# Ternary feed-forward stages: the sums of squares of a half block enter the matmul with ones as one piece

## The reference, cut to what matters

```python
def _ternary_linear(x, w):
    ...
    rms = jnp.sqrt(jnp.sum(x * x, axis=-1, keepdims=True)) / jnp.sqrt(jnp.asarray(d, x.dtype))
    x_norm = x / (rms + EPS)
    return jnp.einsum('bsd,fd->bsf', x_norm, w_q)
h = jax.nn.gelu(_ternary_linear(x, w_up), approximate=False)
return _ternary_linear(h, w_down)
```

## Time and profile before

| | us |
|---|---|
| median of 3 runs | 1459.81 (1459.66 to 1461.78) |
| the profiled execution | 1459.51 |
| its span, first to last instruction | 1457.6 |
| granted TensorE clock, mean | 0.994 |
| PE busy | 1405.6 (96%) |
| VectorE busy | 1059.7 (73%) |
| ScalarE busy | 927.1 (64%) |
| GpSimd busy | 809.0 (55%) |

### The profile page before, as it was taken

How to read it: one execution, slowest core, us unless ns; L and a number is a source line. 1 busy time by engine, 2 the same in 40 slices (tenths; PEclk the granted TensorE clock), 3 DMA queues, 4 the chain that set the end, 5 groups by cost and what they waited for, 6 DMA issues and landing times. The chain is left out here.

```text
span 1457.6 us, 36349 instructions
## 1 busy us (share of the span) xinstructions
PE 1405.6 (96%) x13004; PEld 1169.9 (80%) x13004; DVE 1059.7 (73%) x2347; ACT 927.1 (64%) x1872; POOL 809.0 (55%) x884
## 2 busy tenths in 40 slices
PE   6999999999998999999999999998899999989998
PEld 5777877889896788888889888887677777768886
DVE  6877777565546887776664669775899999966775
ACT  4665565565552655555655558776778887767775
POOL 3766666322113657665552437776666666636774
PEclk9999999999999999999999999999999999999999
DMA  7000000100001000000311010000000000000101
GB/s 228 31 2 1 0 1 2 37 1 1 1 1 58 2 2 1 0 2 2 103 43 29 1 41 1 1 0 1 2 2 0 0 0 0 0 2 10 36 29 44
DMA packets 21176, 26.28 MB, mean 18 GB/s; under 512 B 1984, under 2 KB 19136, under 8 KB 20928
## 3 DMA queue, kind: packets, MB, share of 16 engines
q1 hardware_dynamic: 20768, 24.61, 5.2%
q10 hardware_dynamic: 288, 0.07, 0.0%
HBM read 20.48 MB, written 4.19 MB: 17 GB/s over the span
## 5 line engine op out<-in xcount | busy, mean ns | idle before, releaser
L548 DVE TENSOR_TENSOR ffn_h_lo<-ffn_h,ffn_h_hi 128x512 fp32r<-128x512 f32 x112 | 86.2, 770 | 122.2 <-ACT ffn_h_hi L759 122.2
L758 ACT ACTIVATE ffn_h<-ffn_hp,c_b 128x512 f32<-128x512 f32 x112 | 77.3, 690 | 145.2 <-PE ffn_hp L857 144.7
L548 DVE TENSOR_TENSOR ternary_ffn_h_lo<-ternary_ffn_h,ternary_ffn_h_hi 128x512 fp32r<-128x512 f32 x128 | 110.8, 865 | 76.4 <-ACT ternary_ffn_h_hi L759 76.3
L2218 POOL TENSOR_TENSOR win_rms<-win_sq_sum,win_minus_half 128x20 f32<-128x20 f32 x31 | 109.8, 3540 | 65.0 <-DVE win_sq_sum L2333 65.0
L1253 POOL TENSOR_TENSOR ret_qk<-ret_qk,ret_qk_sin 128x512 f32<-128x512 f32 x64 | 82.7, 1292 | 99.4 <-DVE ret_qk_sin L1360 98.7
L870 PE MATMUL ternary_ffn_yp<-down_ternary,ternary_ffn_h_hi 128*128 128x256 f32 x512 | 132.4, 291 | 0.0
L870 PE MATMUL ternary_ffn_yp<-down_ternary,ternary_ffn_h_lo 128*128 128x256 f32 x512 | 127.7, 282 | 0.0
L870 PE MATMUL ffn_yp<-down_hi,ffn_h_hi 128*128 128x256 f32 x448 | 127.5, 285 | 0.0
L1259 POOL TENSOR_TENSOR ret_rstd<-ret_sums,ret_minus_half 128x16 f32<-128x16 f32 x32 | 103.7, 3240 | 42.7 <-DVE ret_sums L1402 42.7
L870 PE MATMUL ffn_yp<-down_hi,ffn_h_lo 128*128 128x256 f32 x448 | 125.0, 279 | 0.0
L870 PE MATMUL ffn_yp<-down_lo,ffn_h_hi 128*128 128x256 f32 x448 | 125.0, 279 | 0.0
(11 more groups left out here) (331 smaller groups left out, 4683.0 us busy)
## 6 DMA issues: line engine op xcount, KB each, us to landing
staging<-in_w SPq DMA_DIRECT2D x4, 1024.0 KB, 6.1
ffn_x_in<-in_x SPq DMA_DIRECT2D x8, 512.0 KB, 3.7
X<-in_x SPq DMA_DIRECT2D x7, 512.0 KB, 8.0
out<-X SPq DMA_DIRECT2D x7, 512.0 KB, 2.9
staging<-in_wqkv SPq DMA_DIRECT2D x2, 768.0 KB, 4.5
rotary<-in_rotary SPq DMA_DIRECT2D x1, 1024.0 KB, 6.8
staging<-in_w_up SPq DMA_DIRECT2D x1, 1024.0 KB, 5.1
staging<-in_w_down SPq DMA_DIRECT2D x1, 1024.0 KB, 7.6
```

The lines of the kernel that those rows point to most:

```text
L548: nc.vector.tensor_tensor(h_lo[:, m % R, :], h[:, m % R, :], h_hi[:, m % R, :].bitcast(F32), ALU.subtract).then_inc(h_ready, 1)
L758: nc.scalar.activation(h[:, m % R, :], hp[m % 2][:, :], fn, bias=bias)
L2218: nc.gpsimd.tensor_tensor(rms[:, 1, :], sq_sum[:, :], minus_half[:, :], ALU.pow).then_inc(rms_work, 1)
```

## The change

PE no longer takes the two pair sums of a half. VectorE adds them once more, piece 2 into 0 and piece 6 into 4 (`add_halves`), and PE multiplies one piece by ones instead of two: four matmuls in place of eight. The first half's addition stands in VectorE's order after `h_lo` of piece 4 of the same block; the second's after `h_lo` of piece 0 of the next iteration, ahead of `normalise`. PE waits for the new semaphore `halves_added` where it waited for `sq_added`. The second half of a stage's last block is as it was.

```diff
@@ -175,6 +175,7 @@
         w_summed, w_added, total_done = sem("w_summed"), sem("w_added"), sem("total_done")
         limit_done, below_done, made = sem("limit_done"), sem("below_done"), sem("made")
         mix_first, mix_whole, mix_high, ones_set = sem("mix_first"), sem("mix_whole"), sem("mix_high"), sem("ones_set")
+        halves_added = sem("halves_added")
         lo_done, gain_set = sem("lo_done"), sem("gain_set")
         qkv_full, raw_done, sq_done, values_done = sem("qkv_full"), sem("raw_done"), sem("sq_done"), sem("values_done")
         sq_sum_done, head_work, head_scaled = sem("sq_sum_done"), sem("head_work"), sem("head_scaled")
@@ -548,6 +549,13 @@
                 nc.vector.tensor_tensor(h_lo[:, m % R, :], h[:, m % R, :], h_hi[:, m % R, :].bitcast(F32),
                                         ALU.subtract).then_inc(h_ready, 1)
 
+            def add_halves(b, half):
+
+                dve.wait_ge(sq_added, 4 * b + 2 * (half + 1))
+                m = MF // 2 * half
+                nc.vector.tensor_tensor(h_sq[:, m, :], h_sq[:, m, :], h_sq[:, m + 2, :], ALU.add
+                                        ).then_inc(halves_added, 1)
+
             def input_low(b, j, k):
                 dve.wait_ge(xt_read, KD * b + j + 1)
                 full = tp[j][:, :] if ternary else xt[:, j, :]
@@ -711,6 +719,10 @@
                             residual(b - 2, k)
                         if to_do(b):
                             hidden_low(b, m)
+                        if m == 4 and ternary and live(b, NB):
+                            add_halves(b, 0)
+                        if m == 0 and ternary and live(b - 1, NB) and not final_block(b - 1):
+                            add_halves(b - 1, 1)
                         if m == 1 and first_after_begun(g):
                             normalise(g - 1, 1 - k)
                         if m == 0 and ternary and fresh(g - 1):
@@ -894,8 +906,8 @@
                     pe.wait_ge(pool_sq, POOL_SQ * (b + 1))
                     pieces = (4, 5, 6, 7) if adds_late(b) else (4, 6, 7)
                 else:
-                    pe.wait_ge(sq_added, 4 * b + 2 * (half + 1))
-                    pieces = (4 * half, 4 * half + 2)
+                    pe.wait_ge(halves_added, 2 * b + half + 1)
+                    pieces = (4 * half,)
                 if half == 0:
                     at_least(pe, ms_done, b)
                     if at_start(b):
```

## The result

The changed kernel takes 1462.88 us (median of 20 runs, 1461.29 to 1463.80), the kernel before 1459.88 in the same sitting: a ratio of 1.0019, 95% interval 1.0013 to 1.0025. That is 3.0 us slower by the medians, a hair over the 2.9 us that the prediction counted as the same, and 0.19% by the ratio. The interval excludes no change, so this is a small loss and not a draw. The forecast was 1459.9 in a range of 1455.2 to 1464.0. The profiled execution took 1462.72 us with a span of 1460.9, 3.2 us above the one before.

The account below looks back on a forecast made before the run. PE was taken to bound the steady ternary blocks (17.49 us). -6.6 us gain, +3.1 early blocks and +3.9 full blocks gave +0.4 on 1459.51, so 1459.9 us, range 1455.2 to 1464.0.

Parts of the forecast that it names:

- no change that can be told: Whole kernel: stalls and gain cancel to within 2.9 us, 1459.9 us forecast; chance 0.47.
- Two waves a group: PE's 30 record groups: each loses two waves of 0.11 us, 0.22 us a group, 6.6 us won.
- The m = 4 addition costs nothing: First half's addition on VectorE: its wait is empty and it fits idle time of 1.18 us, so no cost.
- Three early blocks: Three blocks where PE already waits for xt_lo: VectorE sets the pace, 1.04 us lost each, 3.1 us together.
- Seven full blocks: Blocks with all the VectorE work: pair sum catches xn and later work stalls PE, 0.55 us each, 3.9 together.
- my worked case of 0.8: Upper bound for a full block, with xn, h_lo and xt_lo delayed by GpSimd: some 0.8 us of stall.
- GpSimd keeps losing: Rival 1: in the seven blocks GpSimd loses each race, no stall, 1456.0 us, floor 1452.9; chance 0.27 with floor.
- Rival 2: VectorE stays late block to block through h_lo 7, 1.82 us instead of 0.69; four blocks add 4.5, 1464.4 us; chance 0.22.
- one wave: Rival 3: PE's groups shorten by only one wave, 0.11 us less a group, 3.3 less won, 1463.2 us; chance 0.04.
- The smallest difference that can be told: Whole kernel's time: a difference under 0.2% (2.9 us) can't be told from none.

Follow-up runs that it names:

- experiment 4: Changed kernel, but GpSimd's first pair sum adds only 8 of 512 columns, so most of piece 1's squares are missing: 1455.85 us, ratio 0.9969.
- experiment 5: Changed kernel without either addition: PE multiplies one piece per half and most pair sums go unadded, so squares are missing: 1458.43 us, ratio 0.9988 against the kernel before.
- experiment 1: Changed kernel with only the first half's addition (m = 4); the second half goes to PE as two pieces: 1458.97 us, ratio 0.9994.
- experiment 6: Only the first half's addition, as in experiment 1, but block 0 of the first ternary stage done as before (two pieces): 1456.54 us, ratio 0.9978.
- experiment 8: Changed kernel, but the additions write a tile of their own and PE waits for them yet still multiplies two pieces: 1464.13 us, ratio 1.0029.
- experiment 3: Changed kernel with the second half's addition one step later, at m = 1, behind xn and h_lo of piece 1: 1463.92 us, ratio 1.0028.
- experiment 7: Experiment 3 with PE asking for the second half's sum one step later (m = 4 in place of 3): 1459.43 us, ratio 1.0001.
- experiment 11: Experiment 5, but block 0 of the first ternary stage keeps two pieces per half: 1458.48 us, ratio 0.9988 against the kernel before.

## Why the prediction was right, and where not

The time lies in the range, 3.0 us above the value, but "no change that can be told" didn't hold: the interval starts at 1.0013. Luck has a part in how near it came. The term for PE's gain is right only where VectorE has slack, the term for the stalls was too small, and of the 3.3 us between the two spans some 1.4 are not the change's.

*Two waves a group, 6.6 us.* The size was right: 296 records in groups of 8, 0.35 us from the group to what follows (0.57 before), 0.44 a block in experiment 4's steady blocks. That PE keeps this once won was the silent premise, and experiment 5 refutes it: alone it is worth 1.5 us. I had asked what VectorE's lateness brings on, and only in one sentence what PE's earliness does.

*The m = 4 addition costs nothing.* Right in steady blocks (17.26 or 17.27 us in experiment 1). In block 0 of the first stage, where VectorE has the weights to prepare, the edit costs 1.5 to 2.4 us by way of block 1 (experiments 1 and 6). Whether that is the addition's price or that of PE's shorter group isn't shown: either alone comes with a long block 1 (20.2 us in experiment 8, 19.8 in experiment 5). I had counted that block as an early one but looked for the cost only in the m = 0 addition.

*Three early blocks, +3.1.* By blocks: first stage 20.21 for 18.16 and 17.42 for 18.01; second 18.20 for 17.49, and 17.26 for 18.01. The sum of the first pair is +1.46 where I had +1.2 (2 x 1.04 less the 0.44 of each); of the second -0.04 where I had +0.16. The total is near, the shape not: the loss falls on one block, and the next gets part of it back. What made block 1 of the first stage long is `h_lo` 2 at 1.77 us, which the sum doesn't name.

*Seven full blocks, 0.55 each.* The mechanism was right in its places: `xn` caught, `h_lo` 1 to its limit, `h_lo` 2 behind the square of piece 3, `xt_lo` late. The size is the term that was too small: 17.78 less 17.05 is 0.73 us, close to my worked case of 0.8 and not to my value; 7 x 0.18 = 1.3 us of the miss, and the last block of the first stage (17.96) adds 0.2. I had counted on races that come out differently from block to block. In the changed kernel they don't: 17.77 or 17.78 us repeats. (In experiments 3, 7 and 8 they alternate.) The `xn` groups show what the Trainium skill ("SBUF — State Buffer", section "SBUF: two separate sides") says: the engine that starts first holds the shared port pair and the other "fully blocks". The trace agrees, 1.39 us to 2.36 with the pair sum from 1386.96 to 1388.35.

*The rest of the 2.8 us between forecast and profile.* The first stage's start, first up matmul to first transposes, took 6.4 us at a granted clock of 0.74, 5.4 at 1.00 before. The change isn't its cause: it is 6.3 at 0.73 in experiment 11, which has no addition, and 5.4 at 1.00 in experiment 8, which has all. 0.4 lie between the stages. Both are differences of single executions; how often the 20 runs had either start is not known, so that the change's own share of the 3.0 us between the medians is not exactly known; between the two profiles it is about 1.9.

*Rivals.* 1 (GpSimd keeps losing): refuted by `xn` at 2.36. 2 (lateness carried from block to block): the carrying is real, and in experiment 5's first stage through the very link I named, `h_lo` 7 at 1.66 us. In the changed kernel `h_lo` 7 takes 0.69 us in the steady block of 1381.86; the circle closes through `xn` and `h_lo` 2 instead, at a lower price than 1.13. 3 (one wave): refuted. Rival 2's price was summed for four blocks, while "from the third of the seven on" would be five.

*The smallest difference that can be told.* Taken as 0.2% from three runs. With 20 runs the interval is 0.06% to either side.

## What to carry to other kernels

Where two engines hold each other up, an edit's cost is not its duration but the phase it gives to what stands behind it: list the instruction pairs that lie within some tenths of a microsecond of a collision, and move time on either engine only with that list. A block that gets shorter on the bounding engine moves every engine's requests forward, and can lose the gain by itself. Of two symmetrical edits try each alone: here one half was free in steady blocks and the other cost more than both gained. Leave out the odd block too, as its neighbours' work differs: doing block 0 of one stage as before won 1.8 to 2.4 us. And read the granted clock of each stretch before a difference between two profiles is put down to the edit.

## What the runs showed of the hardware

- One program ran its steady blocks in two stable patterns, 17.04 and 17.78 us (4%), in two stages of one execution (experiment 5), and the second stage took 138.85 us in experiment 5's profile and 140.99 in experiment 11's with the same instructions. The patterns differ in which engine is first at two places, by 0.2 us at one of them; what decides is open.
- A caught instruction costs much of what catches it: `xn` +0.97 us for a pair sum of 1.39, `h_lo` +0.7 us behind a square of 1.04, and 1.66 us instead of 0.69 behind a late pair sum.
- GpSimd's pair sum itself got shorter when it no longer lost races: 1.39 us at 1386.96 beside 1.71 before, and 1.46 us in the mean of its 61 instances beside 1.55. An engine's own instructions got faster while the kernel became slower.
- At the start of the first stage the granted clock was 1.00 in four profiles (5.4 us to the first transposes) and 0.73 or 0.74 in the nine others (6.3 to 6.4 us). PE had sat idle for 2.4 us before its first matmul there in all thirteen. The edit didn't decide it: kernels with and without additions are in both groups.
